# A fused decoder layer: second softmax shifted by a product with -I, FFN rows turned by transfers, inner norms folded away, free PSUM banks

## The reference, cut to what is computed

```python
# attention 1 (16 heads of 16, 64 latents)
attn_logits = einsum('bhtd,lhd->bhtl', Q, latent) / sqrt(HD)
topk_logits, topk_idx = top_k(attn_logits, 4)
weighted = softmax(topk_logits) @ selected latents
out1 = (weighted + V) @ Wo.T + bo
x = layernorm(x + out1)
# attention 2 (16 heads, rope on the context, low-rank weights)
scores = einsum('bhsr,bhlr->bhsl', q_r, k_r)
out2 = softmax(scores) @ kv_rope -> w_kc_kv -> Wo.T
x = layernorm(x + out2)
# FFN, each linear: rmsnorm, round to 8 bits, ternary weight
h = silu(linear_bit(x, w1, g1)) * linear_bit(x, w2, g2)
x = layernorm(x + linear_bit(h, w3, g3))
```

## Time and profile before

| | us |
|---|---|
| median of 3 runs | 366.58 (366.23 to 367.68) |
| span of the profiled execution | 364.8 |
| TensorE in work | 335.7 |
| VectorE in work | 311.2 |
| ScalarE in work | 261.4 |
| GpSimd in work | 247.4 |

### The profile page before, as it was taken

One profiled execution on the slowest core, in us unless ns is written; L12 is line 12 of the kernel. 1 busy time (PEld: TensorE's weight loads), 2 busy tenths in 40 slices (PEclk: granted clock), 3 DMA queues, 4 the chain that ended last, 5 costly groups with the idle time before them and its releaser, 6 DMA issues.

```text
span 364.8 us, 7459 instructions
## 1 busy us (share of the span) xinstructions
PE 335.7 (92%) x2549; PEld 249.6 (68%) x2549; DVE 311.2 (85%) x776; ACT 261.4 (72%) x467; POOL 247.4 (68%) x223
## 2 busy tenths in 40 slices
PE   8889998997799879999899989899999999998684
PEld 4587785785677557777677767677877778666342
DVE  2763467699979999989989999999999898998984
ACT  2536898972758549867889778578998588688762
POOL 3263725679976588794984959478879746768551
PEclk9969999999989999999999999999999999999999
DMA  7999920000000000000000000000000000000001
GB/s 214 237 364 362 368 109 2 0 3 1 2 0 2 1 3 0 2 0 17 6 11 16 1 1 2 16 15 3 2 14 3 14 16 0 16 16 14 5 27 44
DMA packets 6597, 17.58 MB, mean 48 GB/s; under 512 B 864, under 2 KB 3680, under 8 KB 5728
## 3 DMA queue, kind: packets, MB, share of 16 engines
q1 hardware_dynamic: 6560, 17.11, 13.9%
HBM read 15.01 MB, written 2.10 MB: 47 GB/s over the span
## 4 chain that ended last, share of the span: by engine, by line
PE 43%; DVE 19%; POOL 18%; issue 12%; DMA 4%; ACT 2%; SPq 1%; POOLq 0%; DVEq 0%; ACTq 0%
PE wide L501 6%; PE small L539 6%; DMA region_c<-in_wkcqT 4%; PE wide L560 3%; PE wide L485 3%; PE wide L516 3%; POOL region_c L1344 3%; PE wide L434 3%; PE wide L422 2%; DVE m L997 2%; PE small L457 2%; POOL P L1320 2%; PE wide L334 2%; POOL Ls L1300 2%; PE wide L527 2%
## 5 line engine op out<-in xcount | busy, mean ns | idle before, releaser
L539 PE MATMUL small<-V_sb,PT_sb 128*128 128x256 f32 x256 | 58.7, 382 | 1.5 <-DVE y_row L1028 1.5
L539 PEld LDWEIGHTS small<-V_sb,PT_sb 128*128 128x128 f32 x256 | 47.6, 190 | 9.7 <-DVE y_row L1028 2.3
L1285 POOL TENSOR_TENSOR Ls<-Ls,m 128x1024 f32<-128x1024 f32 x16 | 31.4, 1961 | 28.2 <-DVE mask L1011 28.2
L501 PE MATMUL wide<-B_sb,x1T 128*128 128x512 f32 x192 | 49.6, 407 | 0.0
L1344 POOL TENSOR_TENSOR region_c<-region_c,region_q 128x1024 f32<-128x1024 f32 x16 | 33.2, 2072 | 16.4 <-DVE region_c L1135 13.6
L501 PEld LDWEIGHTS wide<-B_sb,x1T 128*128 128x128 f32 x192 | 35.5, 188 | 9.8 <-issue 1.4
L1292 POOL TENSOR_TENSOR mask<-mask,r 128x1024 f32<-128x1024 f32 x16 | 31.5, 1967 | 15.4 <-DVE r L1020 15.4
L1300 POOL TENSOR_TENSOR Ls<-Ls,mask 128x1024 f32<-128x1024 f32 x16 | 38.0, 2372 | 2.7 <-ACT Ls L753 2.0
L997 DVE MAX8 m<-Ls 128x8 f32<-128x64 f32 x256 | 33.9, 208 | 4.8 <-ACT Ls L740 4.7
L1320 POOL TENSOR_TENSOR P<-P,r 128x1024 f32<-128x1024 f32 x16 | 32.1, 2007 | 8.6 <-DVE r L1075 8.6
L560 PE MATMUL wide<-tern,region_k 128*128 128x512 bf16 x128 | 31.8, 379 | 0.9 <-ACT region_k L837 0.7
(11 more groups left out here) (177 smaller groups left out, 882.2 us busy)
## 6 DMA issues: line engine op xcount, KB each, us to landing
xT<-in_xT SPq DMA_DIRECT2D x8, 256.0 KB, 8.8
region_q<-in_wqx SPq DMA_DIRECT2D x1, 2048.0 KB, 17.7
region_c<-in_woTx SPq DMA_DIRECT2D x1, 2048.0 KB, 7.3
out_x<-region_q SPq DMA_DIRECT2D x16, 128.0 KB, 1.7
region_c<-in_wkcqT SPq DMA_DIRECT2D x2, 768.0 KB, 12.6
region_r<-in_w1T SPq DMA_DIRECT2D x1, 1024.0 KB, 11.0
region_t<-in_w2T SPq DMA_DIRECT2D x1, 1024.0 KB, 13.0
w_raw<-in_w3T SPq DMA_DIRECT2D x1, 1024.0 KB, 15.0
```

Source lines behind the costliest of these rows:

```text
L501: mm = pe.matmul(ps_L2[:, r * 512:(r + 1) * 512], x1T[:, u, k, :], B_sb[:, s, w, k, r * 512:(r + 1) * 512], start=(u == w == k == 0), stop ...
L539: mm = pe.matmul(ps_O2[:, 0:D], PT2_sb[:, c, :], V_sb[:, c, :], start=(c == 0), stop=(c == PAIRS - 1))
L1285: pool.tensor_tensor(heads(Ls[n % 2][:]), heads(Ls[n % 2][:]), over_heads(m8[:, :, 0:1]), ALU.subtract).then_inc(g_d1, 1)
```

## The change

1. The second softmax. `shift_2` goes. A new `S2(n)` adds to the logits, where they lie in PSUM, a product of `minus_ident` (-I, fp32r) with the maxima spread over 64 columns. `exp_2` reads PSUM, and its scale is the first norm's root.
2. Inner norms. `norm_1`, `norm_2` and `square_x2` go. The rows `y1` before the norm are kept in six homes, transposed and multiplied as they are; the root comes in as the scale of `exp_2`, and `residual_2` multiplies the second attention's output by the deviation (`sd1`). `roots_1` and `roots_2` make two and three powers at once; `moments_2` is a small step on VectorE. W3's ternary matrix is centred once (`centre_3`), so that the last norm needs no mean: `square_3` and `norm_3` are on ScalarE, `moments_3` is one small step.
3. FFN rows. `whole_x` and `whole_h` round, and new `pack_x` and `pack_h` write fp16. For tiles 0 to 11 (`TURNED = 12`) SyncE turns them by a transposing transfer from SBUF to SBUF; tiles 12 to 15 keep `XQT`, `copy_XQ`, `HT`, `copy_HT`.
4. Banks and buffers. PSUM becomes four pairs (`wide`), and tables give each step of each tile its home. Two homes each for `th`, `hh`, `hg`, `xg`, `xqT`, `hqT`, `x1T`, `m8`, `d4`, `PT1_sb`, `AT`. `O1` is parted: `XW` (the part with x) may come earlier.
5. `V_` has 8 products of 512 columns per sequence instead of 16 of 256.
6. Loads. Several are joined (`front`, `lat`, `context`, `t1w`, the later parts of xT): three stand ahead of `wkcqT` where nine did, and the context table comes after `wv1`.
7. All five lists are written anew. `warm` has 56 products, 30 of them at the head.

```diff
-        wide = [ctx.enter_context(nc.psum_tensor(f"wide{k}", [P, WIDE], F32)) for k in range(3)]
+        wide = [ctx.enter_context(nc.psum_tensor(f"wide{k}", [P, WIDE], F32)) for k in range(4)]
...
+TURNED = 12
+HOME_L2 = (3, 1, 1, 1, 3, 0, 2, 3, 1, 0, 0, 0, 2, 1, 3, 1)
...
+            def turn_x(n):
+                sp.wait_ge(a_px, n + 1)
+                since(sp, p_Z2, n - 1)
+                sp.dma_start_transpose(xqT[n % 2], xq16[n % 2]).then_inc(t_x[n % 2], 16)
+            def turn_h(n):
+                sp.wait_ge(a_ph, n + 1)
+                since(sp, p_O3, n - 1)
+                sp.dma_start_transpose(hqT[n % 2], hq16[n % 2]).then_inc(t_h[n % 2], 16)
...
+            turn_x(0); turn_x(1); turn_x(2); turn_x(3); turn_h(0); turn_h(1); turn_x(4); turn_h(2)
+            turn_x(5); store(0); turn_h(3); store(1); turn_x(6); turn_x(7); turn_h(4); turn_h(5)
...
+            def S2(n):
+                pe.wait_ge(v_max2, n + 1)
+                for r in range(2):
+                    rows = m2[n % 2][:, r * PAIRS:(r + 1) * PAIRS].rearrange("p (h o) -> p h o", o=1)
+                    mm = pe.matmul(pair(HOME_L2, n)[:, r * 512:(r + 1) * 512].rearrange("p (h l) -> p h l", l=L),
+                                   minus_ident[:], rows.to_broadcast([P, PAIRS, L]), start=False, stop=True,
+                                   skip_group_check=True)
+                mm.then_inc(p_S2, 1)
...
             def Z_(w, n, *freed):
-                pe.wait_ge(a_qT, n + 1)
+                if n < TURNED:
+                    pe.wait_ge(t_x[n % 2], 16 * (n // 2 + 1))
+                else:
+                    pe.wait_ge(a_qT, n - TURNED + 1)
...
+            L2(8, v_bl, 12); L2(9, v_g1, 6); X1T(10); S2(8); WT(12, v_g2, 6); S2(9); O3(2, v_xlo, 11)
...
+            WT(15, v_y1, 15); Z_(0, 10, a_V1, 7); S2(12); X1T(14, v_y3, 8); XW(15, a_AT, 16); L2(13)
+            Z_(1, 10, a_ex2, 13); Z_(0, 11, v_g1, 11); S2(13); O1(15); Z_(1, 11, v_g2, 11)
...
             def exp_2(n):
-                act.wait_ge(v_sub2, n + 1)
-                act.activation(P2_sb[n % 2][:], P2_sb[n % 2][:], ACT.Exp).then_inc(a_ex2, 1)
+                act.wait_ge(p_S2, n + 1)
+                act.wait_ge(g_rt1, n + 1)
+                act.activation(P2_sb[n % 2][:], pair(HOME_L2, n), ACT.Exp, scale=root1[n]).then_inc(a_ex2, 1)
...
+            def pack_h(n):
+                act.wait_ge(a_qh, n + 1)
+                act.activation(hq16[n % 2], hg[n % 2], ACT.Copy, bias=-ROUND).then_inc(a_ph, 1)
+            def square_3(n):
+                act.activation(junk_3[:, 0:D], y2[n % Y2_HOMES], ACT.Square, scale=D ** -0.5,
+                               accum_out=var3[n]).then_inc(a_sq3, 1)
+            def norm_3(n):
+                act.activation(x3[n % 2], y2[n % Y2_HOMES], ACT.Copy, scale=root3[n]).then_inc(a_ln3, 1)
...
+            whole_h(7); tanh(9); square_h(8); pack_h(7); copy_X1(13); copy_V(1, 6); square_h(9)
+            square_1(14); whole_x(11); pack_x(11); copy_PT1(15); copy_AT(15); square_3(7); tanh(10)
...
-            def shift_2(n):
-                dve.tensor_tensor(heads(P2_sb[n % 2][:]), heads(ps_L2[:]),
-                                  over_heads(m2[:].rearrange("p (h o) -> p h o", o=1)), ALU.subtract
-                                  ).then_inc(v_sub2, 1)
...
+                dve.scalar_tensor_tensor(y2[n % Y2_HOMES], bank(HOME_O2, n)[:, 0:D], sd1[n], y1[n % Y1_HOMES],
+                                         ALU.mult, ALU.add).then_inc(v_y2, 1)
```

1091 lines of the change are left out of this document (530 added, 561 removed).

## The result

The changed kernel takes **374.65 us** (median of 4 runs, 372.24 to 375.25) where the kernel before takes 366.40 in the same session: a ratio of **1.0212, interval 1.0164 to 1.026: slower, by some 2%**. The forecast was 359, faster. The profiled execution took 372.24 us, 370.5 of it the span; as in the kernel before, 1.7 us lie around it.

A forecast was written before the change was run, and what follows sets the result against it. TensorE was taken as the steady stage's bound, VectorE close behind. TensorE's work to the last O2 311.7, standing 11.7 and tail 34 sum to 357.4; with 1.8 around the span, 359 us, range 347 to 377.

The forecast's parts named there:

- GpSimd keeps its large operations; its roots move, under its 32% of idle time: GpSimd's list: large operations stay and moved roots fit its idle time; no term in the sum.
- late transfers: Rival: Z and O3 of tiles 0 to 11 wait on TensorE for turning transfers, 18 us, 377 us; chance 0.13.
- a late S2: Rival: S2 in TensorE's queue waits for VectorE's maxima, 22 us in place of 3, 378 us; chance 0.10.
- the standing time: TensorE's waits up to the last O2: 18.2 us fall to 11.7, ramp and steady stage halved, 3 new for S2.
- nothing comes of it: Rival: TensorE's standing time moves elsewhere instead of halving, 366 us, because four fixed queues wait on each other; chance 0.10.
- TensorE's work: TensorE's busy time up to the last O2: 316.4 us becomes 311.7 through transposes, maxima products, V and order.
- the upper end 0.41: S2's 32 products on TensorE: 0.26 us each taken, 8.3 in all; 0.41 each if alone, 13.0 in all.
- The tail: After the last O2: ScalarE has 26.5 us listed; 34 us taken, between 29.7 and 40.3, 4 longer than before.
- The head's 2.5 us for wkcqT: TensorE's wait in the head for the load wkcqT, 2.5 us, goes because fewer loads stand ahead of it.
- the case of 666 us: Rival: issuing a tile's pair of turning transfers takes an estimated 41 us and decides the time, 666 us; chance 0.02.
- VectorE as the gate: Rival: VectorE filled 94% of the steady stage; relieved, its standing goes and the tail is short, 347 us; chance 0.13.
- the rule that one goes by the fullest engine: Rival's further case: VectorE, busy 85%, is fullest, so its 39 us less the tail's 4 come off, 331 us; chance 0.03.

The follow-up runs named there:

- e9: Changed kernel with GpSimd's atanh series in four pieces, the last piece, weights and roots_2(0) ahead of scale_mask(7): 366.18 us, ratio 1.0039.
- e4: Kernel before the change, with its atanh series and weights moved into one block ahead of gain_x(0) and shift_1(6): 371.23 us, ratio 1.0109.
- e16: e9 without the 32 products of S2 and without VectorE's 16 maxima of the second softmax: 364.64 us, ratio 0.9993.
- e17: e9 without GpSimd's 16 scale_mask multiplications, which scale the first softmax's mask: 355.89 us, ratio 0.9731.
- after: The changed kernel as first measured, with every part of the change, against the kernel before: 374.65 us, ratio 1.0212.
- e13: e9 with TensorE also making the transposes that the transfers replaced, nobody waiting for them: 368.14 us, ratio 1.0061.
- e6: Changed kernel with another order of the head: weights_1(0) sooner on GpSimd, Q(1) and XW(0) ahead of PT1(1) on TensorE: 373.26 us, ratio 1.0171.
- e10: e9 with the head's order of e6 as well: 366.43 us, ratio 1.0014.
- e14: e9 with each of the 24 transfers made twice, one behind the other, products waiting for the second: 366.89 us, ratio 0.9997.
- e7: Changed kernel with VectorE's max_2(4) and max_2(5) put sooner in its list: 373.51 us, ratio 1.0194.
- e12: e9 with the second softmax's subtraction back on VectorE and no S2 products: 379.50 us, ratio 1.0380.
- e1: Changed kernel with GpSimd's atanh series and weights moved behind shift_1(6) and roots_1(4), still ahead of shift_1(7): 373.96 us, ratio 1.0227.
- e5: Changed kernel with GpSimd's atanh series cut into four pieces, the last, the weights and roots_2(0) behind weights_1(7): 373.30 us, ratio 1.0197.

## Why the prediction was wrong

**The step that failed** is the one on GpSimd: "GpSimd keeps its large operations; its roots move, under its 32% of idle time". It counted GpSimd's work and never walked its list, though the list was in the diff and a shift that VectorE, ScalarE and TensorE need stood newly behind the series and its weights, 13 of the block's 18 us. That omission is, within the noise, the whole loss against the kernel before: 8.5 us by e9's median, 6.3 by its ratio, and 4.0 us by e4 in the other kernel. None of the four rivals named it. Nor had the sum a term for the clock, in which 3.1 of the 5.2 us lie that the profiles show for it. That 374.65 us lies inside the stated range is luck: the range reached up there for late transfers and a late S2, and neither made it.

**The second failed step** is the standing time: "I halve both", for the ramp's 9.7 and the steady stage's 4.4 us, because VectorE and the banks were relieved. With the block mended (e9) TensorE stands 333.9 - 311.8 = 22.1 us where 11.7 were forecast and the kernel before had 18.2: 9.9 in the ramp, 7.3 in the steady stage. Another 4.9 lie outside these two, where 1.6 were forecast. The waits did not go with VectorE's work: sparing VectorE 15.6 us more (e16) left 26.7 us. They went with GpSimd's: 32.1 us off its list (e17) left 13.9 us, near the forecast. So the rival "nothing comes of it", with 366 and a chance of 0.10, is what the rest of the change did, by the mechanism given there; that its number is met to 0.2 us is partly luck, since its sum has 18.7 us of standing and a tail of 34 where e9 has 22.1 and 29.4.

**TensorE's work** came out right in sum: 311.7 forecast, 311.8 in e9; 316.7 in after, which holds the slow stretches behind the two holes (clock 0.83 and 0.91). But it was a sum of errors that met, and it was not worth what the forecast took it for. The groups of after by line, against the earlier trace rows (busy us, mean ns):

```profile
L549 PE MATMUL wide<-C_sb,context 64*64 64x512 f32 x128 | 18.1, 642 | 0.0
L326 PE MATMUL wide<-zeros 128*128 128x512 bf16 x53 | 14.7, 422 | 1.5 <-DVE zeros L1213 1.2 <-issue 0.2
L535 PE MATMUL wide<-m,minus_ident 128*128 128x512 f32 x32 | 12.4, 471 | 4.4 <-DVE m L1114 4.3
L606 PE MATMUL wide<-ident,w_raw 128*128 128x128 f16 x32 | 2.4, 219 | 2.2 <-ACT w_raw L900 2.2
L581 PE MATMUL wide<-ident,region_k 128*128 128x128 f16 x16 | 1.5, 219 | 2.5 <-ACT region_k L860 2.5
```

S2 took 12.4/32 = 0.39 us each, near the upper end 0.41 and not the 0.26 of the sum: 12.4 us instead of 8.3 (11.6 in e9). V gained nothing (18.1 against 17.5 us). Against these stand gains that no term named: in e9 the products with wkcqT took 3.7 us instead of 7.1 and Q 15.3 instead of 17.7. The transposes fell by 7.4 and 4.7 us as summed, but a group's time is not what it adds: e13 put all of them back and the busy time rose by 8.8, not 12.0, and the time by 2.5 or less. That neighbouring groups overlap at their edges would explain the 8.8; no run shows it apart. Here the sum of the groups' times overstated what leaving them out could give.

**The tail** was 29.4 us, not 34. ScalarE has 24.35 of the 26.5 us listed there, and runs nearly through; the lower end, 29.7, was the right one.

**The other terms.** The head's 2.5 us for wkcqT did go (the product starts at 17.6 us), and waits of 1.39 and 1.59 us for GpSimd came behind it; clearing these by another order showed no gain by tile 10 (e6, e10). ScalarE has 275.9 us, forecast 274. VectorE has 284.9 where 311.2 - 39 = 272 were forecast; the next section has a part of the difference.

**The rivals.** Late transfers: false, 2.4 and 2.7 us where the store gave 1.7 and 3.4, and hidden even at twice that (e14); a tile's pair landed in 5.1 us in all, so issuing never decided, and the case of 666 us is false too. S2 waiting for a late VectorE: the waits are there, 4.3 us, but cut to 1.0 (e7) they gave nothing alone. VectorE as the gate: false as written, since less VectorE work brought at most 1.7 us (e16); more of it does cost (e12). On the rule that one goes by the fullest engine, the Trainium skill (Perfetto Trace Analysis, "Identifying the Most-Contended Engine") says to improve the engine with the highest occupancy first, weight loads standing in for TensorE. By e9's shares that is VectorE, 78%, with GpSimd at 71%. The runs do not agree here: 15.6 us off VectorE with 4.2 off TensorE gave at most 1.7 us, 32.1 us off GpSimd gave 10.3. In this kernel the shares did not point at the engine whose list paid; TensorE's and ScalarE's waits for GpSimd did.

What stays open: what holds the piece from tile 10 to the last O2 at 182.5 to 183.7 us in every order tried. In e9 TensorE works 176.2 us of it, at a clock of 1.00, and yet in e16, with 5.7 us less of that work, the piece is only 2.8 us shorter. Taking work away (e16, e17: 180.1 and 180.5) or adding it changed it. No run gave ScalarE less to do, which by the change has 14.5 us more than before (275.9 against 261.4), so its list stands as an untested rival there.

## What to carry to other kernels

A change that rewrites the engines' lists has to be costed list by list: for every step that moves, name what stands behind it and who waits for that, on the idle engines too. An edit that fills one hole must be judged at a later mark that all orders share (here the scores of tile 10): in e1, e5 and e7 the standing only moved to another engine's wait. Before summing what an engine is spared, put the work back idle on it once, or leave it out once; here TensorE's transposes and S2 were worth about a quarter of their busy time or less.
